# Attention probabilities of four units in ten split before they are turned, and turned by DMA

## The reference, cut to what matters

```python
latents = x @ W_down.T                       # 64 wide
keys, values = latents @ W_uk.T, latents @ W_uv.T
q = x @ W_q.T                                # 16 heads of 128
scores = einsum('bhqd,bhkd->bhqk', q, k) / sqrt(128)
scores = where(causal, scores, -inf)
attn = softmax(scores)
ctx = einsum('bhqk,bhkd->bhqd', attn, v)
return ctx @ W_o.T
```

## Time and profile before

| | |
|---|---|
| median of 3 runs | 259.3 us (257.52, 259.3, 259.41) |
| the profiled execution | 257.85 us, its span 256.1 us |
| busy over the span | PE 238.5 (93%), DVE 209.0 (82%), ACT 168.0 (66%), POOL 70.5 (28%) |
| attention loop | about 70 to 200 us, a pass 16.2 us |
| granted TensorE clock | 1.00 throughout |

### The profile page before, as it was taken

One profiled execution on the slowest core, in us unless ns is written; L12 is line 12 of the kernel. 1 busy time (PEld: TensorE's weight loads), 2 busy tenths in 40 slices (PEclk: granted clock), 3 DMA queues, 4 the chain that ended last, 5 costly groups with the idle time before them and its releaser, 6 DMA issues.

```text
span 256.1 us, 7254 instructions
## 1 busy us (share of the span) xinstructions
PE 238.5 (93%) x2627; PEld 180.5 (71%) x2650; DVE 209.0 (82%) x499; ACT 168.0 (66%) x322; POOL 70.5 (28%) x124
## 2 busy tenths in 40 slices
PE   6699897999889999999999999999998899998995
PEld 2554356985758878878788787787887788754364
DVE  3868789987768999989999999999999437378783
ACT  2747762275787888879889798897988400355740
POOL 5220146000002435433444434344355000300310
PEclk9999999999999999999999999999999999999999
DMA  6999200001201103416034160341506420000005
GB/s 225 237 315 367 39 0 4 0 3 34 50 0 44 45 9 77 79 41 123 0 81 83 41 123 0 72 93 41 111 19 78 44 41 3 0 0 4 0 0 166
DMA packets 34793, 17.22 MB, mean 67 GB/s; under 512 B 25484, under 2 KB 34520, under 8 KB 34520
## 3 DMA queue, kind: packets, MB, share of 16 engines
q1 hardware_dynamic: 33576, 15.81, 27.5%
q10 hardware_dynamic: 1200, 1.18, 1.4%
HBM read 7.55 MB, written 1.05 MB: 34 GB/s over the span
## 4 chain that ended last, share of the span: by engine, by line
PE 68%; DVE 19%; ACT 4%; DMA 3%; issue 3%; SPq 1%; DVEq 0%
PE bank L1065 12%; PE bank L850 9%; PE bank L1140 8%; PE bank L878 7%; PE bank L1056 7%; PE bank L1055 4%; PE bank L1079 3%; DMA cT<-in_L_ffn_w_dram 3%; PE bank L1078 3%; PE bank L973 3%; PE bank L1080 3%; PE bank L1012 3%; PE bank L1057 2%; DVE pT_lo L754 2%; DVE nmax L749 2%
## 5 line engine op out<-in xcount | busy, mean ns | idle before, releaser
L501 ACT ACTIVATE prob<-bank,nmax 128x384 f32<-128x384 f32 (+3 forms) x128 | 62.2, 527 | 8.3 <-DVE nmax L745 6.8
L754 DVE TENSOR_TENSOR pT_lo<-bank,pT_hi 128x512 f16<-128x512 f32 x80 | 54.7, 684 | 3.1 <-ACT pT_hi L507 2.4
L507 ACT CAST pT_hi<-bank 128x512 f16<-128x512 f32 x80 | 46.7, 584 | 11.1 <-PE bank L1065 10.7
L1065 PE MATMUL bank<-ident,prob 128*128 128x128 f32 x320 | 50.5, 280 | 0.6 <-ACT prob L501 0.6
L384 POOL TENSOR_TENSOR cst<-craw,rsum 128x256 f32<-128x256 f32 x30 | 18.4, 612 | 95.0 <-DVE craw L763 95.0
L1078 PE MATMUL bank<-lat,pT_hi 128*128 128x65 bf16 x320 | 37.7, 193 | 2.3 <-DVE pT_lo L754 2.3
L1079 PE MATMUL bank<-lat,pT_hi 128*128 128x64 bf16 x320 | 37.8, 195 | 0.0
L1056 PE MATMUL bank<-latT_lo,wqo 128*128 128x384 bf16 (+3 forms) x128 | 36.6, 299 | 1.2
L1080 PE MATMUL bank<-lat,pT_lo 128*128 128x65 bf16 x320 | 37.5, 192 | 0.0
L1078 PEld LDWEIGHTS bank<-lat,pT_hi 128*128 128x128 f16 x320 | 30.1, 96 | 7.2 <-DVE pT_lo L754 2.0
L745 DVE TENSOR_REDUCE nmax<-bank 128x1 f32<-128x512 f32 (+1 forms) x48 | 32.7, 683 | 1.9 <-PE bank L1057 1.9
(11 more groups left out here) (173 smaller groups left out, 472.0 us busy)
## 6 DMA issues: line engine op xcount, KB each, us to landing
wqo<-stage SPq DMA_DIRECT2D x64, 64.0 KB, 2.1
wqo<-in_L_attn_W_q_dram SPq DMA_DIRECT2D x1, 2048.0 KB, 9.3
wqo<-in_L_attn_W_o_dram SPq DMA_DIRECT2D x1, 2048.0 KB, 14.8
out_dram<-X SPq DMA_DIRECT2D x8, 128.0 KB, 1.9
X<-in_L_attn_x_dram ACTq DMA_DIRECT2D x1, 512.0 KB, 7.0
cT<-in_L_attn_W_uk_dram SPq DMA_DIRECT2D x1, 512.0 KB, 10.8
cT<-in_L_attn_W_uv_dram SPq DMA_DIRECT2D x1, 512.0 KB, 10.7
cT<-in_L_ffn_w_dram SPq DMA_DIRECT2D x1, 384.0 KB, 4.9
```

The costliest lines, as they stand in the source:

```text
L501: last = nc.scalar.activation(prob[:, u % 2, cols], bank[SCORE_BANK[u]][:, cols], ACT.Exp, bias=nmax[:, u, n:n + 1])
L507: nc.scalar.copy(pT_hi[:, j % 2, :], bank[3 + j % 2][:, :]).then_inc(pThi_ready, 1)
L754: nc.vector.tensor_tensor(pT_lo[:, j % 2, :], bank[3 + j % 2][:, :], pT_hi[:, j % 2, :], ALU.subtract).then_inc(pTlo_ready, 1)
L1065: last = nc.tensor.transpose(bank[3 + j % 2][:, blk(k)], prob[:, j % 2, blk(k)], ident[:, :])
```

## The change

Units 1, 3, 6 and 8 of each pass (`BY_DMA`) are no longer turned by TensorE. ScalarE casts their exponentials to the high part right behind the exponent (`high_part`), GpSimd subtracts for the low part (`low_part`), and SP turns both parts with two transposing DMAs of 128x512 elements (`turn_probabilities`) into `turned`, which the context product reads. `prob` has five buffers, the parts and `turned` two each. The other six units go as before, with their own count of buffers and semaphores.

Scores run seven units ahead instead of four (`LEAD`), maxima with them and exponents six. The query products of pair i+2 run in steps 8 and 10 of pass i, those of pair 1 before the first scores. Unit 9's scores leave bank 7. SP's order is written anew; GpSimd's subtractions stand between its divisions. VectorE's steps follow the same numbers.

```diff
...
-    SCORE_BANK = [0, 1, 7, 2, 0, 1, 2, 0, 1, 7]
-    HELD_BY = [-3, -2, -1, -4, 0, 1, 3, 4, 5, None]
+    SCORE_BANK = [0, 1, 7, 2, 0, 1, 2, 0, 1, 2]
+    HELD_BY = [-3, -2, None, -1, 0, 1, 3, 4, 5, 6]
+    LEAD = 7
+    BY_DMA = [1, 3, 6, 8]
+    BY_PE = [u for u in range(UNITS) if u not in BY_DMA]
+    ND, NPE = len(BY_DMA), len(BY_PE)
+    PROBS = 5
...
-        prob = sb("prob", [P, 2, SEQ], F32)
+        prob = sb("prob", [P, PROBS, SEQ], F32)
+        prob_hl = sb("prob_hl", [P, 2, 2, SEQ], FP16)
+        turned = sb("turned", [P, 2, 2, SEQ], FP16)
...
+            def move_queries(i, t):
+                sp.wait_ge(u_lo, i * 2 + (t + 1))
+                for side in range(2):
+                    for part in range(2):
+                        sp.dma_start(uc[LAT * part:LAT * (part + 1), i * 2 + side:i * 2 + side + 1, tokens(t)],
+                                     stage[LAT * side:LAT * (side + 1), part:part + 1, tokens(t)]).then_inc(u_moved[t], 16)
+
+            def turn_probabilities(i, j):
+                d = in_order(BY_DMA, i, j)
+                sp.wait_ge(prob_lo, d + 1)
+                if d >= 2:
+                    sp.wait_ge(turned_used, d - 1)
+                for part in range(2):
+                    sp.dma_start_transpose(turned[:, d % 2, part, :].rearrange("p (k q) -> p k q", k=SB),
+                                           prob_hl[:, d % 2, part, :]).then_inc(prob_turned[d % 2], 16)
+
+            for i in range(2):
+                for t in range(2):
+                    move_queries(i, t)
+            for j in BY_DMA[:2]:
+                turn_probabilities(0, j)
             for i in range(NP):
-                for t in range(2):
-                    sp.wait_ge(u_lo, i * 2 + (t + 1))
-                    for side in range(2):
-                        for part in range(2):
-                            sp.dma_start(uc[LAT * part:LAT * (part + 1), i * 2 + side:i * 2 + side + 1, tokens(t)],
-                                         stage[LAT * side:LAT * (side + 1), part:part + 1, tokens(t)]).then_inc(u_moved[t], 16)
-                if i >= 2:
-                    sp.wait_ge(clo_ready, B + 2 * B * (i - 1))
-                    transpose_context(i - 2, 0, NB, cT_early)
-            sp.wait_ge(clo_ready, B + 2 * B * (NP - 1))
-            transpose_context(NP - 2, 0, NB, cT_mid)
+                turn_probabilities(i, 6)
+                if 0 < i < NP - 1:
+                    move_queries(i + 1, 1)
+                turn_probabilities(i, 8)
+                if i > 0:
+                    sp.wait_ge(clo_ready, B + 2 * B * i)
+                    transpose_context(i - 1, 0, NB, cT_mid if i == NP - 1 else cT_early)
+                if i < NP - 1:
+                    turn_probabilities(i + 1, 1)
+                    turn_probabilities(i + 1, 3)
+                if i < NP - 2:
+                    move_queries(i + 2, 0)
...
+            def low_part(i, j):
+                d = in_order(BY_DMA, i, j)
+                r = BY_DMA.index(j % UNITS) % 2
+                pool.wait_ge(prob_hi, d + 1)
+                if not (isinstance(i, int) and i == 0 and j in BY_DMA[:2]):
+                    pool.wait_ge(prob_turned[r], i * (16 * ND) + 32 * ((j // UNITS * ND + BY_DMA.index(j % UNITS)) // 2))
+                nc.gpsimd.tensor_tensor(prob_hl[:, r, 1, :], prob[:, j % PROBS, :], prob_hl[:, r, 0, :],
+                                        ALU.subtract).then_inc(prob_lo, 1)
+
+            for j in (1, 3, 6):
+                low_part(0, j)
             with pool.Fori(0, NP - 1) as i:
-                for side in range(2):
-                    divide_context(i, side)
-            divide_context(NP - 1, 0)
+                low_part(i, 8)
+                divide_context(i, 0, 0)
+                low_part(i, UNITS + 1)
+                divide_context(i, 0, 1)
+                low_part(i, UNITS + 3)
+                divide_context(i, 1, 0)
+                low_part(i, UNITS + 6)
+                divide_context(i, 1, 1)
+            low_part(NP - 1, 8)
+            for b in range(B):
+                divide_context(NP - 1, 0, b)
...
+                if (u - PROBS) % UNITS in BY_DMA and not (isinstance(i, int) and i == 0 and j < PROBS):
+                    act.wait_ge(prob_lo, in_order(BY_DMA, i, j - PROBS) + 1)
                 for n, (b, q, at) in enumerate(HEAD_UNITS[u % HU]):
                     cols = slice(at, at + P * (q + 1))
-                    last = nc.scalar.activation(prob[:, u % 2, cols], bank[SCORE_BANK[u]][:, cols], ACT.Exp,
+                    last = nc.scalar.activation(prob[:, u % PROBS, cols], bank[SCORE_BANK[u]][:, cols], ACT.Exp,
...
+            def high_part(i, j):
+                d = BY_DMA.index(j % UNITS)
+                act.wait_ge(prob_ready, i * UNITS + (j + 1))
+                if not (isinstance(i, int) and i == 0 and j in BY_DMA[:2]):
+                    act.wait_ge(prob_turned[d % 2], i * (16 * ND) + 32 * ((j // UNITS * ND + d) // 2))
+                nc.scalar.copy(prob_hl[:, d % 2, 0, :], prob[:, j % PROBS, :]).then_inc(prob_hi, 1)
...
             def attention_step(i, j, queries=True):
-                if not beyond(i, j + 3):
-                    exponent(i, j + 3)
-                if queries and j in (1, 3):
-                    split_queries(i + 1, j // 2)
-                if not beyond(i, j + 2):
+                if not beyond(i, j + LEAD - 1):
+                    exponent(i, j + LEAD - 1)
+                    if (j + LEAD - 1) % UNITS in BY_DMA:
+                        high_part(i, j + LEAD - 1)
+                if queries and j in (8, 10):
+                    split_queries(i + 2, (j - 8) // 2)
+                if not beyond(i, j + 2) and (j + 2) % UNITS in BY_PE:
                     split(i, j + 2)
...
+            for t in range(2):
+                split_queries(1, t)
+            for j in range(LEAD - 1):
+                exponent(0, j)
+                if j in BY_DMA:
+                    high_part(0, j)
...
-                if not (isinstance(i, int) and t == 0):
+                if not (isinstance(i, int) and i == 0 and t == 0):
                     pe.wait_ge(u_lo, i * 2 + t)
+                if not isinstance(i, int) and t == 0:
+                    pe.wait_ge(prob_ready, i * UNITS - UNITS + 3)
...
-                unit = j % HU
...
-                pe.wait_ge(pTlo_ready, i * UNITS + (j + 1))
+                if u in BY_DMA:
+                    d = BY_DMA.index(u)
+                    pe.wait_ge(prob_turned[d % 2], i * (16 * ND) + 32 * ((j // UNITS * ND + d) // 2 + 1))
+                    parts = [turned[:, d % 2, part, :] for part in range(2)]
+                else:
+                    pe.wait_ge(pTlo_ready, in_order(BY_PE, i, j) + 1)
+                    parts = [p[:, BY_PE.index(u) % 2, :] for p in (pT_hi, pT_lo)]
...
+                if u in BY_DMA:
+                    last.then_inc(turned_used, 1)
...
             def attention_step(i, j, with_queries=True):
-                if with_queries and j in (1, 3):
-                    queries(i + 1, j // 2)
-                if not beyond(i, j + 4):
-                    scores(i, j + 4)
+                if with_queries and j in (8, 10):
+                    queries(i + 2, (j - 8) // 2)
+                if not beyond(i, j + LEAD):
+                    scores(i, j + LEAD)
                 context(i, j)
-                if not beyond(i, j + 2):
+                if not beyond(i, j + 2) and (j + 2) % UNITS in BY_PE:
                     transposes(i, j + 2)
...
+            for t in range(2):
+                queries(1, t)
             pe.wait_ge(lat_lo, 3)
-            for j in range(3):
+            for j in range(LEAD):
                 scores(0, j)
-            pe.wait_ge(n_lo, 4)
-            transposes(0, 0)
-            scores(0, 3)
-            transposes(0, 1)
-            attention_step(0, 0)
-            with pe.Fori(0, NP - 1) as i:
-                for j in range(1, UNITS + 1):
+                if j == 2:
+                    pe.wait_ge(n_lo, 4)
+                    transposes(0, 0)
+            for j in range(8):
+                attention_step(0, j)
+            with pe.Fori(0, NP - 2) as i:
+                for j in range(8, 8 + UNITS):
                     attention_step(i, j)
+            for j in range(8, 8 + UNITS):
+                attention_step(NP - 2, j, with_queries=False)
...
```

More of the change, by code:

```diff
@@ L237, in bass_macaron_moe_mla_moe @@
         prob_ready = sem("prob_ready")
+        prob_hi = sem("prob_hi")
+        prob_lo = sem("prob_lo")
+        prob_turned = [sem(f"prob_turned{r}") for r in range(2)]
+        turned_used = sem("turned_used")
         pT_ps = sem("pT_ps")
@@ L274, in blk, with in_order @@
             return slice(n * P, (n + 1) * P)
+        def in_order(units, i, j):
+            assert j % UNITS in units
+            return i * len(units) + (j // UNITS * len(units) + units.index(j % UNITS))
         def beyond(i, j):
@@ L488, in split_queries @@
```

(41 more changed lines are left out.)

66 lines of the change are left out of this document (37 added, 29 removed).

## The result

The changed kernel takes **286.79 us** (median of 4, 283.89 to 288.31) against 258.88 of the kernel before: a ratio of 1.1046, 95% interval [1.0986, 1.1107]. Forecast were 266 and at most 279. The sign was right, the size was not. The profiled execution took 288.31 us, its span is 286.2.

The account below looks back on a forecast made before the run. SP's DMA issue queue was taken as the bound, 17.65 us a pass. Start, five full passes, a short one and the end put the output product at 208.1 against 200.4, +7.7: 265.5, said as 266 us; range 257 to 279.

Parts of the forecast that it names:

- The nearest bound: In the loop, SP's queue of DMA issues sets the pace: 17.65 us a pass, against TensorE's new 14.34.
- Rival 1: On SP, transposing issues cost about 0.60 us, so TensorE's shorter pass comes through: about 249 us; chance 0.16.
- rival 2: On SP, a transposing pitch near 1.08 us gives passes of 16.2, matching the old: 258.3 or 259 us; chance 0.10.
- rival 3: Stalls on SP or in tight loops, as one issue of four took 2.41 us: 272 to 280 us; chance 0.13.
- The start: Before the loop, both query products of the second pair precede the first scores: costs 4 us, bounded by 2 and 7.
- SP's sum: SP's issues in one pass: eight transposes 10.1, query moves 4.8, context transposes 2.75, together 17.65 us.
- The other loop: Moves landed, scores, maximum, exponent, high part, low part, turns and moves: about 17.2 us, perhaps costing a few tenths a pass.
- both just in time: SP needs contexts 8 and 11 at 12.65 and 17.65 us of a pass; they end at 12.2 and 17.1.
- a sign of being wrong: The prediction is wrong if SP idles in mid-loop or its transposes issue in under 0.9 us.
- TensorE's granted clock is no fourth: No rival for TensorE's clock: it stayed 1.00 when busy 6.72 of 10 us; here busy about 14.2 of 17.65.
- The end: After five full SP passes: a short pass of 15.25 us, last turns and landing 6.2, last contexts about 7.0, ending at 208.1.
- Behind the output product: After the last context, products keep TensorE busy 7.9 us and the last context transposes land inside it; no added time.

Follow-up runs that it names:

- run 1: Changed kernel with one transposing DMA of 128x1024 for each turned unit in place of two of 128x512: 274.25 us, 1.0601 of the kernel before.
- run 4: Changed kernel with no unit turned by DMA, all ten transposed on TensorE; lead of seven, five buffers of prob and new order kept: 264.06 us, 1.0234.
- run 2: Changed kernel, same DMAs, with the second half's four query moves issued ahead of the turn of unit 6: 282.74 us, 1.0928.
- run 3: Changed kernel with 16 extra unused matmuls of 248 columns on TensorE before it waits for the query moves: 283.5 us, 1.0934.
- run 5: Changed kernel with one transposing DMA a turned unit and the second half's query moves ahead of the turn of unit 6: 273.77 us, 1.0556.
- run 6: run 5 with four buffers in place of two for the split and the turned probabilities: 276.15 us, 1.0642.
- 10: run 7 with ScalarE's high part behind the cast of its step, the exponent still first: 263.54 us, 1.0183.
- run 7: run 6 with two units' scores ahead of pair 1's first query products, and unit 0's first split ahead of exponents of units 2 to 5: 276.4 us.
- 15: Kernel of 10 with five scores and a transpose ahead of pair 1's query products at the start, and two buffers for turned units, not four: 265.37 us, 1.0284.

## Why the prediction was wrong, step by step

**What it had right.** The nearest bound: in the pass of 18.43 SP's queue ran without a gap, and the turning issues took about what was foretold (1.22), by their shortest, median and longest in ns:

```profile
L331 SPq DMA_TRANSPOSE turned<-prob_hl x41: 1188/1259/1377, 101.8 to 199.7; - x41
```

The sums of the engines: GpSimd 11.18 a pass (11.4 foretold), ScalarE 13.83 (13.96), VectorE 13.18 (12.7); TensorE 15.20 (14.34), the least exact; that sum starts from 16.22, which no row has, and the busy 16.07 of the earlier trace rows would give 14.2. The DMA engines: 0.56 x 18.43 = 10.3 against 10.2. The rule of the Trainium skill (DMA: Bandwidth & Descriptors, section Issuing engines are not separate DMA queues) that the time to start a DMA is usually small beside the DMA itself is again not what the trace shows: 1.25 us of issue against about 0.7 of transfer, and run 1, which halves the number of turning issues for the same bytes, won 12.5 us. Rival 1 (issues near 0.60), rival 2 (pitch 1.08) and rival 3's reason (one issue in four stalls) all fell with the same rows.

**What failed.** The forecast's span was 256.1 + 7.7 = 263.8, the measured one is 286.2: 22.4 to explain, by the prediction's own marks. The bound was right in kind. What failed is its size, the waits and the clock that were put at nothing beside it, and above all the start and the end.

1. *The start:* turn 16 at 97.6; measured 101.83, **+4.2**. With the 4 foretold that makes a start of 8.2, above the bound given (2 to 7). The two products and their splits were priced one by one; run 4 shows that the order costs 5.9, by the first context, even with no DMA. The rest came with the turns; from 82 to 84 us the granted clock was 0.50 here too.
2. *SP's sum:* 17.65 a pass; measured 18.43, and 18.39 bare in run 2. Five passes, **+3.9**. Most of it is the moves: four were taken at 2.4, their busy time, where from start to start they need 2.61 to 2.69. The 0.04 us between neighbours was counted for transposes only, and from one kind of DMA to the next it is 0.05 to 0.19. This term had its own upper end of 18.7 in the text, with a pitch of 1.39 where the row gives 1.36 (18.4); it was only mis-sized.
3. *The other loop,* "any can cost a few tenths a pass", and SP's waits for contexts, "both just in time": four of five passes took 1.2 to 2.1 longer than SP's sum, 97.84 - 5 x 18.43, **+5.7**. In these passes SP did idle in mid-loop, 4.5 us in all, which the prediction had named as a sign of being wrong. It waited for contexts, which TensorE brought late behind the landing of the moves; the chain through the high part and the low part is as long. The step that failed is the sentence "TensorE's granted clock is no fourth". The half clock was given no price, and the four long passes are those in which it fell to 0.50. The sentence was read from ten microseconds whose longest wait on TensorE was 1.87 us:

```profile
7.28 1.50 PE L987 MATMUL bank<-ident,cT 128*128 128x128 f32 x12 [1.87 <-DMA cT<-in_L_ffn_w_dram]
```

   In the loop it stood 2.20 us before the scores in four passes and 3.53 in the first. The stand alone is not the rule, since one of the four left the clock at 1.00. Run 2 gave the loop slack, run 3 kept the clock up, and the late passes of both came to 18.4.
4. *The end:* from the fifth pass's end to the output product 22.3; measured 29.53, **+7.2**. The last units run with no scores left to fill TensorE: clock 0.87 over the stretch, 0.50 from 222 us on. The chain of waits there shows a landing 5.04 us after the second issue of a turn began, and then cast and subtraction of one unit after another, with TensorE waiting:

```profile
212.84 1.22 SPq L331
...
214.11 5.04 DMA turned<-prob_hl
...
224.01 0.59 ACT pT_hi L574
224.63 0.70 DVE pT_lo L830
```

   The forecast took 3.7 from a turn's first issue to its landing, where this one took 6.3 (212.84 to 219.15), and gave the last units' hand-overs no time of their own. What each is worth was not tried alone, so the cause of this term, the largest, stays open.
5. *Behind the output product* 57.0 in place of 55.7, **+1.3**, at a mean clock of 0.98; the forecast left this part as it was.

These make 22.3. The range reached only to 279 because stalls were priced as one rival with one cause; several terms that went the same way were not added up.

**What the prediction never saw.** It took SP for the one obstacle and TensorE's 14.34 for what lay behind. Run 1 shows another at once: with SP's sum at 13.2 us the pass is 17.33, not 14.34. Runs 5, 6 and 10 name it: neither moves nor buffers, but a loop over VectorE and ScalarE, maximum, exponent, high part, cast, subtraction, a later maximum, that the order of two instructions on ScalarE set. By pass, the two causes together read:

| | high part, then cast | cast, then high part |
|---|---|---|
| two DMAs a unit | 18.4 to 20.5 | 20.7 |
| one DMA a unit | 17.33 | 15.65 |

Neither edit alone is enough, and one of them alone is harmful. (The right column's lower entry has moves first, four buffers and the start of run 7, too; runs 5, 6, 7 and 15 show that these leave the pass as it is with one DMA a unit. With two DMAs they were not tried together with the new order.) With both, the transposes that left TensorE are at last worth 0.6 us a pass, 3 to 4 us over the kernel, which the longer start takes back. That the loop goes exactly through the instructions named is read from the waits and the program order; that the order of these two sets the pass was shown.

## What to carry to other kernels

Add up a DMA-issuing queue from start to start, hand-overs included, as one would a compute engine; then close every loop that runs through it and add its latencies. When work is moved to another engine, ask where its instruction lands in that engine's program order and who waits behind it: here that was worth as much as the DMAs. A wait in the profile is a cause only if the time falls when it goes: run 6 removed SP's waits for contexts (17.3 us in run 1, 9.7 in run 5) and won nothing.

## What the runs showed of the hardware

- The granted clock fell to 0.50 within a loop that had run at 1.00, up to 1.5 us after TensorE had stood 2.20 us before its scores (changed kernel, passes from 122.34, 141.96 and 180.03). The same stand of 2.20 us in the pass from 161.60 left it at 1.00. What else decides is not shown.
- A clock of 0.91 cost nothing where TensorE was off the path: run 2's passes are 18.39 at either.
- A transposing DMA of twice the columns took the same time to issue: 1.23 us in the median for 128x1024 in run 1, 1.26 for 128x512 in the changed kernel. One DMA in place of two gave back half of the time that a turn takes in the queue (1.28 from start to start against 2.55).
